# A two-layer transformer-and-SSM kernel: quantisation through PSUM ring banks, a router that reads PSUM, and a new table of slots

## The reference, cut to what matters

```
attention:  softmax((x*w_lhs) @ (x*w_rhs).T) @ x
fp8 layer:  x_q = (bf16(x) / s_in).astype(float8_e4m3fn)
            y   = (x_q @ k_q) * (s_in * s_k), in bf16, plus bias
SSM:        in_proj, causal convolution over 4 taps, silu,
            scan over 512 steps with 16 states for 512 channels, gate, out_proj
MoE:        scores = softmax(x @ gate_w.T) over 8 experts, the best 2 per token,
            their silu-gated products, weighted by the score,
            plus a shared expert times a sigmoid gate
```

## Time and profile before

| | us |
|---|---|
| median of 3 runs | 3776.05 (3775.61 to 3776.88) |
| the profiled execution, its own time | 3764.44 |
| its span, first to last instruction | 3762.7 |
| the first stage | until about 3030 |
| mean granted TensorE clock | 0.899 of full speed |

### The profile page before, as it was taken

How to read it: one execution, slowest core, us unless ns; L and a number is a source line. 1 busy time by engine, 2 the same in 40 slices (tenths; PEclk the granted TensorE clock), 3 DMA queues, 4 the chain that set the end, 5 groups by cost and what they waited for, 6 DMA issues and landing times. The chain is left out here.

```text
span 3762.7 us, 46426 instructions
## 1 busy us (share of the span) xinstructions
PE 2964.0 (79%) x12696; PEld 1908.2 (51%) x12697; DVE 2680.7 (71%) x4101; ACT 2032.6 (54%) x3738; POOL 2645.6 (70%) x2497
## 2 busy tenths in 40 slices
PE   3676868787877878787878696878687759999997
PEld 1444544554554545545454454554545436666665
DVE  2498898989898989898988888888988522222221
ACT  2566656666665657575656666656565313333332
POOL 1389887888888888888887878788899523333333
PEclk8897989889888989898989898989897879999998
DMA  2010111111111110101010101111011053333332
GB/s 67 21 32 28 38 35 36 35 34 37 34 35 34 37 40 31 43 30 41 28 43 32 40 32 37 35 37 36 30 39 37 25 148 55 53 53 53 53 53 44
DMA packets 113257, 155.35 MB, mean 41 GB/s; under 512 B 15601, under 2 KB 72369, under 8 KB 113073
## 3 DMA queue, kind: packets, MB, share of 16 engines
q1 hardware_dynamic: 72624, 99.79, 8.7%
q0 software_dynamic: 26112, 35.81, 5.5%
q10 hardware_dynamic: 14336, 17.57, 1.5%
HBM read 107.36 MB, written 45.76 MB: 41 GB/s over the span
## 5 line engine op out<-in xcount | busy, mean ns | idle before, releaser
L785 POOL TENSOR_TENSOR dbu<-du,bbc 128x512 f32<-128x512 f32 x1024 | 1298.3, 1280 | 129.2 <-DVE h L1269 120.1
L1269 DVE TENSOR_TENSOR_SCAN h<-bank,dbu 128x512 f32<-128x512 f32 x1024 | 1221.6, 1210 | 150.4 <-PE bank L609 67.2
L980 ACT ACTIVATE bank<-delta,amat 128x512 f32<-128x512 f32 x1024 | 704.2, 690 | 532.1 <-DVE h L1269 526.9
L609 PE MATMUL bank<-ident,h 128*128 128x128 f32 x4096 | 643.2, 294 | 403.2 <-DVE acc L1259 378.3
L609 PEld LDWEIGHTS bank<-ident,h 128*128 128x128 f32 x4096 | 512.7, 152 | 704.0 <-DVE acc L1259 366.1
L771 POOL TENSOR_TENSOR acc<-acc,hTc 128x512 f32<-128x512 f32 x480 | 611.2, 1273 | 184.8 <-ACT hTc L964 182.8
L1472 POOL DMA_INDIRECT out<-ye,ids x136 | 213.5, 1570 | 450.3 <-issue 236.1
L964 ACT ACTIVATE hTc<-bank,cT 128x512 f32<-128x512 f32 x480 | 326.9, 681 | 270.8 <-PE bank L609 268.5
L563 PE MATMUL bank<-x4T,w_su 128*128 128x512 f32 (+1 forms) x768 | 430.2, 656 | 0.0
L1519 DVE SCALAR_TENSOR_TENSOR gg<-gt,bank 128x352 f32<-128x352 f32 x136 | 70.9, 521 | 500.3 <-ACT gt L1422 500.3
L1259 DVE SCALAR_TENSOR_TENSOR acc<-bank,cT,acc 128x512 f32<-128x512 f32 x544 | 393.5, 728 | 18.4 <-PE bank L609 16.8
(11 more groups left out here) (197 smaller groups left out, 4522.3 us busy)
## 6 DMA issues: line engine op xcount, KB each, us to landing
bbc<-b_scratch SPq DMA_DIRECT2D x256, 256.0 KB, 3.1
xe<-slots_in SPq DMA_DIRECT2D x136, 129.0 KB
x<-in_x SPq DMA_DIRECT2D x16, 512.0 KB, 3.9
out<-x ACTq DMA_DIRECT2D x16, 512.0 KB, 3.0
w_gu<-in_e_gu ACTq DMA_DIRECT2D x8, 704.0 KB
out<-ye,ids POOLq DMA_INDIRECT x136, 3.8
slots_in<-x,pos POOLq DMA_INDIRECT x128
w_dn<-in_e_dn ACTq DMA_DIRECT2D x16, 128.0 KB
```

What stands on the lines that cost most here:

```text
L609: last = tr(scan[f"hT{s}.{t}"][:, m * P:(m + 1) * P], h[:, s % 2, m, t * P:(t + 1) * P], ident[:, :])
L785: g.tensor_tensor(dbu[:, n % 4, :], du[:, m, :], bbc[:, (b * NS + s) % NROW, :], ALU.mult).then_inc(S("dbu_ready"), 1)
L980: f(db(n)[:, :], delta[:, par, m, :], ACT.Exp, scale=amat[:, m, s:s + 1]).then_inc(S("da_ready"), 1)
L1269: v.tensor_tensor_scan(h[:, s % 2, m, :], db(n)[:, :], dbu[:, n % 4, :], 0.0, ALU.mult, ALU.add)\
```

## The change

- **Quantisation.** The working value `qm` lies in two ring banks, each with half of the tile; `reserve` takes them in TensorE's order at slot `q_dve` with no fill, `take` lets VectorE wait for their former readers. VectorE does each step in two halves of 128x512: exponent bits and magic (slot 57), then add and subtract in their new forms. ScalarE forms the overflow product from PSUM into SBUF (`q_nan`=56), and VectorE makes the last add into `qb` (`q_fin`=58). GpSimd has no part in it.
- **Router.** The logits are read from PSUM with no copy, the exponentials are written to another part of the same bank; the indices go to float by a reduction over one element instead of a cast; the running count starts from `run`, which is now row 0 of `cum`, so that its copy goes; the sums are written to the count's bank and cast from there. The logit bank is held until the scores, the count bank until the positions are made.
- **Slots.** The table `AT` is set anew, some forty entries, most by one or two slots.

```diff
+    def reserve(self, name, b):
+
+        self.free.sort()
+        bank = self.free.pop(0)[2]
+        turn, slot = self.due[name]
+        self.at[name, b] = (bank, self.fills[bank])
+        self.before[name, b] = self.last[bank]
+        self.free.append((b + turn, slot, bank))
+        self.last[bank] = (name, b)
+
+    def take(self, eng, name, b, done):
+
+        earlier = self.before[name, b]
+        if earlier:
+            for sem, i in self.readers[earlier[0]]:
+                done(eng, sem, earlier[1], i)
...
+        cum = psb("cum", [P, TT, E])
+        run = cum[:, 0, :]
...
-            yT=(0, 0, 1, 1), y=(1, 1, 1, 1), uD=(2, 2, 3, 3), acc0=(1, 2, 2, 3), out=(4, 6), x3=(8, 10), stats5=11, rstd5=11, x4=14,
-            x4T_pe=(14, 16), x4T=(15, 18), logit=18, lg=20, lexp=20, score=26, route=28, count=39, place=41,
-            ranks=(42, 43, 44, 45, 50, 51, 52, 53), g_pe=(20, 26, 30, 40, 44, 50), g=(22, 27, 32, 41, 46, 51),
-            gate=(24, 29, 34, 43, 48, 53), u_pe=(23, 26, 33, 42, 47, 54), up=(25, 29, 36, 45, 50, 54), d_pe=(51, 56), fin=(59, 66),
-            stats3=2, rstd3=1, res=3, r4=4, r4T_pe=5, r4T=4, in_x=(8, 10, 15, 17), tap=(11, 12, 17, 19), conv=(13, 15, 19, 21),
-            tanh=(13, 15, 20, 21), u=(16, 17, 22, 24), base=12, xBC_pe=24, bs=26, cT_pe=27, cT=32, in_z=(31, 38, 44, 51),
-            z=(34, 40, 47, 53), zs=(36, 41, 48, 55), dt_pe=(26, 34, 40, 46), raw=(30, 38, 44, 50), sp_exp=(32, 41, 46, 52), sp_ln=50,
-            delta=(53, 54, 55, 56), stats1=4, rstd1=4, xn=8, xT=(9, 12), xl=(11, 12), scores=(15, 19, 21, 26), maxs=(18, 21, 25, 29),
-            probs=(18, 21, 25, 29), probT_pe=(30, 33, 34, 35), probT=(32, 34, 36, 39), av=(40, 48), x1=(45, 53), stats2=47, rstd2=51,
-            xb=54, q=52, q_dve=56, q_add=56, qT_pe=61, qT=62, ffn_pe=(62, 63), ffn=(63, 64), x2=64, store=1, tags=(41, 50))
+            yT=(0, 0, 1, 2), y=(0, 0, 1, 1), uD=(2, 3, 3, 3), acc0=(1, 2, 2, 2), out=(4, 6), x3=(7, 10), stats5=12, rstd5=11, x4=14,
+            x4T_pe=(14, 16), x4T=(14, 16), logit=17, lg=20, lexp=20, score=21, route=26, count=39, place=40,
+            ranks=(42, 45, 45, 47, 50, 51, 52, 54), g_pe=(20, 26, 30, 40, 44, 50), g=(22, 27, 32, 41, 46, 51),
+            gate=(24, 29, 34, 43, 48, 53), u_pe=(23, 25, 33, 42, 44, 54), up=(25, 29, 36, 45, 51, 56), d_pe=(51, 56), fin=(58, 63),
+            stats3=2, rstd3=1, res=3, r4=4, r4T_pe=5, r4T=3, in_x=(8, 10, 15, 17), tap=(11, 12, 17, 19), conv=(13, 15, 19, 21),
+            tanh=(13, 15, 20, 21), u=(16, 17, 23, 24), base=12, xBC_pe=24, bs=25, cT_pe=29, cT=31, in_z=(31, 38, 45, 51),
+            z=(33, 40, 48, 53), zs=(38, 43, 50, 55), dt_pe=(26, 34, 40, 49), raw=(30, 38, 44, 52), sp_exp=(32, 44, 49, 55), sp_ln=51,
+            delta=(54, 55, 56, 56), stats1=4, rstd1=4, xn=8, xT=(9, 11), xl=(11, 12), scores=(15, 19, 21, 26), maxs=(18, 21, 25, 29),
+            probs=(18, 21, 24, 29), probT_pe=(30, 33, 34, 36), probT=(32, 34, 36, 37), av=(40, 47), x1=(46, 52), stats2=48, rstd2=51,
+            xb=54, q=50, q_dve=57, qT_pe=56, qT=62, ffn_pe=(63, 63), ffn=(63, 64), x2=64, store=0, tags=(40, 54), q_round=54, q_nan=56,
+            q_fin=58)
...
+        for k in range(2):
+            attn.add(f"qm{k}", -2, AT["q_fin"], ("q_ready", 0))
...
-        late.add("logit", 1, AT["lg"], ("lg_ready", 0))
-        late.add("count", 1, AT["place"], ("slot_ready", None))
+        late.add("logit", 1, AT["score"], ("score_ready", None))
+        late.add("count", 1, AT["place"], ("pos_ready", 0))
...
+        def router_views(b):
+
+            bank = late["logit", b]
+            return (bank[:, 0:TT * (E + 1)].rearrange("p (t e) -> p t e", e=E + 1),
+                    bank[:, P:P + TT * E].rearrange("p (t e) -> p t e", e=E))
...
+                yield AT["q_dve"]
+                for k in range(2):
+                    attn.reserve(f"qm{k}", b)
...
-                yield AT["q_add"]
-
-                done(pool, "q_nan", b)
-                g.tensor_tensor(qb[:, :, :], qm[:, :, :], qs[:, :, :], ALU.add).then_inc(S("q_ready"), 1)
...
+                yield AT["q_nan"]
+                done(act, "q_rounded", b)
+                for k in range(2):
+                    last = f(qm[:, 2 * k:2 * k + 2, :], attn[f"qm{k}", b][:, :].rearrange("p (j d) -> p j d", j=2), ACT.Copy, scale=3.4e38 / 460.0)
+                last.then_inc(S("q_nan"), 1)
...
+                    f(sg[:, :], given[:, :, E], ACT.Exp, scale=-1.0).then_inc(S("sg_ready"), 1)
                     f(lexp[:, :, :], lsub[:, :, :], ACT.Exp).then_inc(S("lexp_ready"), 1)
-                    f(sg[:, :], lg[:, :, E], ACT.Exp, scale=-1.0).then_inc(S("sg_ready"), 1)
...
-                names = SHARED["q_step"][1:]
-                to_e4m3(qs[:, :, :], qm[:, :, :], lambda n: done(dve, names[n], b), [S(n) for n in names])
+                quants = [(qs[:, 2 * k:2 * k + 2, :], attn[f"qm{k}", b][:, :].rearrange("p (j d) -> p j d", j=2),
+                           qm[:, 2 * k:2 * k + 2, :], qb[:, 2 * k:2 * k + 2, :]) for k in range(2)]
+                for k in range(2):
+                    attn.take(dve, f"qm{k}", b, done)
+                for q, m, _, _ in quants:
+                    last = v.tensor_scalar(m.bitcast(i32), q.bitcast(i32), 0x7F800000, None, ALU.bitwise_and)
+                last.then_inc(S("q_expo"), 1)
+                done(dve, "q_expo", b)
+
+                for q, m, _, _ in quants:
+                    last = v.tensor_scalar(m, m, 2.0 ** -6, 1.5 * 2.0 ** 20, ALU.max, ALU.mult)
+                last.then_inc(S("q_magic"), 1)
+                yield AT["q_round"]
+                done(dve, "q_magic", b)
+                for q, m, _, _ in quants:
+                    last = v.tensor_tensor(q, m, q, ALU.add)
+                last.then_inc(S("q_added"), 1)
+                done(dve, "q_added", b)
+                for q, m, _, _ in quants:
+                    last = v.scalar_tensor_tensor(m, m, -1.0, q, ALU.mult, ALU.add)
+                last.then_inc(S("q_rounded"), 1)
+                yield AT["q_fin"]
+                done(dve, "q_nan", b)
+                for q, m, big, rounded in quants:
+                    last = v.scalar_tensor_tensor(rounded, big, 0.0, m, ALU.mult, ALU.add)
+                last.then_inc(S("q_ready"), 1)
...
-                    v.tensor_copy(lg[:, :, :], late["logit", b][:, 0:TT * (E + 1)].rearrange("p (t e) -> p t e", e=E + 1)).then_inc(S("lg_ready"), 1)
-                    done(dve, "lg_ready", b)
-                    v.tensor_reduce(lmax[:, :], lg[:, :, 0:E], AX.X, ALU.max).then_inc(S("lmax_ready"), 1)
+                    v.tensor_reduce(lmax[:, :], given[:, :, 0:E], AX.X, ALU.max).then_inc(S("lmax_ready"), 1)
                     done(dve, "lmax_ready", b)
-                    v.tensor_tensor(lsub[:, :, :], lg[:, :, 0:E], lmax[:, :].unsqueeze(2).broadcast_to([P, TT, E]), ALU.subtract)\
+                    v.tensor_tensor(lsub[:, :, :], given[:, :, 0:E], lmax[:, :].unsqueeze(2).broadcast_to([P, TT, E]), ALU.subtract)\
...
-                    v.tensor_copy(f8[:, :, :], i8[:, :, :]).then_inc(S("idxf_ready"), 1)
+                    v.tensor_reduce(f8[:, :, :], i8[:, :, 0:2].unsqueeze(3), AX.X, ALU.max).then_inc(S("idxf_ready"), 1)
...
-                    v.tensor_copy(cum[:, 0, :], run[:, :]).then_inc(S("cum0"), 1)
+                    if b > 0:
+                        done(dve, "run_ready", b - 1)
                     for j in range(1, TT):
-                        done(dve, f"cum{j - 1}", b)
-                        v.tensor_tensor(cum[:, j, :], cum[:, j - 1, :], tiles[:, j - 1, :], ALU.add).then_inc(S(f"cum{j}"), 1)
+                        if j > 1:
+                            done(dve, f"cum{j - 1}", b)
+                        v.tensor_tensor(cum[:, j, :], tiles[:, j - 1, :], cum[:, j - 1, :], ALU.add).then_inc(S(f"cum{j}"), 1)
                     done(dve, f"cum{TT - 1}", b)
-                    v.tensor_tensor(run[:, :], cum[:, TT - 1, :], tiles[:, TT - 1, :], ALU.add).then_inc(S("run_ready"), 1)
-                    v.tensor_tensor(slot[:, :, :], cum[:, :, :], within, ALU.add).then_inc(S("slot_ready"), 1)
+                    v.tensor_tensor(slot[:, :, :], within, cum[:, :, :], ALU.add).then_inc(S("slot_ready"), 1)
                     done(dve, "slot_ready", b)
+                    v.tensor_tensor(run, tiles[:, TT - 1, :], cum[:, TT - 1, :], ALU.add).then_inc(S("run_ready"), 1)
                     v.tensor_tensor(ohb[:, :, :, :], ohb[:, :, :, :], slot[:, :, :].unsqueeze(1).broadcast_to([P, 2, TT, E]), ALU.mult)\
                         .then_inc(S("prod_ready"), 1)
                     done(dve, "prod_ready", b)
-                    v.tensor_reduce(posf[:, :, :], ohb[:, :, :, :], AX.X, ALU.add).then_inc(S("posf_ready"), 1)
+                    posf = late["count", b][:, P:P + 2 * TT].rearrange("p (w t) -> p w t", w=2)
+                    v.tensor_reduce(posf, ohb[:, :, :, :], AX.X, ALU.add).then_inc(S("posf_ready"), 1)
```

(2 more changed lines are left out.)

22 lines of the change are left out of this document (11 added, 11 removed).

## The result

The kernel after the change takes 3544.85 us (median of 4 runs, 3531.26 to 3554.79) beside 3775.83 us of the kernel before: 0.939 times, 95% interval 0.9356 to 0.9425. The profiled execution of after has a span of 3542.6 us, against 3762.7: 220.1 us less.

A forecast was written before the change was run, and what follows sets the result against it. VectorE was taken as the bound, 87% busy in a 180.8 us turn. Terms 70 - 1 + 40 + 37 = 146 us, less 14, gave 132 off 3764.4, 3632; plus 11.6, 3644 us, range 3590 to 3730.

The forecast's parts named there:

- Gain 5.4 us a turn: Quantisation on VectorE: 11.7 us removed, 6.3 us added per turn; over 13 turns 70 us, less 1 at the start.
- The last add leaving GpSimd: Quantisation: GpSimd loses its add of 2.34 us; not taken as a gain of its own, bounds 0 and 2.34.
- The other shifts: Slots: z and zs two slots later, y at 0, touch waits of 1.7 us and less; nothing taken.
- I take off a tenth: Whole sum: some freed time will end at GpSimd's adds, with GpSimd 86% busy; 14 us taken off 146.
- The late up product: Slots: VectorE's 4.89 us wait for TensorE's last up product; about half saved, 2.5 us x 15 turns = 37 us.
- the forecast's second remark: Slots: the last softplus exponential moves to 55, putting ScalarE's logarithm block under VectorE's quantisation; laid bare it costs 72 us.
- The router: Router copies and casts removed or reading PSUM: 3.1 us a turn, 2.5 taken, x 16 = 40 us, bounds 0 and 50.
- first rival: The holds move to VectorE instructions with two SBUF inputs: router gains nothing, 74 us in all, 3702 us; chance 0.10.
- Second rival: Slower: in-order stall as TensorE waits at slot 57 for the quantised tile; in full 3840 us; chance 0.07.
- Fourth: PSUM at single rate, no hold lifted: 22 us dearer, router 0, 3761 us, or no change; chance 0.05.
- more than forecast, all upper bounds: Whole kernel: every term at its upper bound, time below 3590 us; chance 0.03.
- The bounds of the terms: Largest gains allowed: quantisation 107 us, router 50 us, slots 99 us (6.6 us a turn).

The follow-up runs named there:

- q_only: The kernel before with only the quantisation's new code, router and slots as they were; 3680.27 us, ratio 0.9756.
- score21: The kernel before with only the score's slot moved from 26 to 21; 3728.75 us, ratio 0.9875.
- r_only: The kernel before with the router's new code and the score's slot moved from 26 to 21; 3694.54 us, ratio 0.9794.
- qr_oldslots: The kernel before with the new quantisation and router code on the old slots, with the edits of q_only and r_only; 3585.33 us, ratio 0.9501.
- q_hold: q_only with the quantisation's first pass as before, one instruction from SBUF to SBUF; 3767.26 us, ratio 0.998.
- qr_up: qr_oldslots with the last two up products moved from slots 50 and 54 to 51 and 56; 3615.36 us, ratio 0.9571.
- qr_tail: qr_up with the last softplus exponential moved from slot 52 to 55, its product and raw copy to 49 and 52; 3593.59 us, ratio 0.9526.
- s_only: The kernel before with only the new slots, quantisation and router code as before; 3644.43 us, ratio 0.9661.
- place_only: The kernel before with only the second half of the router's code (running counts and positions); 3726.1 us, ratio 0.9869.
- rest_only: The kernel after with the last up products, last softplus exponential, its product and raw copy back on old slots; 3627.88 us, ratio 0.9617.
- after_hold: The kernel after with the quantisation's first pass as before, one instruction from SBUF to SBUF; 3544.55 us, ratio 0.9401.

## Why the prediction was wrong

The sign and the main mechanism, the lifted hold, were right, the size was not. The sum goes against the runs as follows, in the order in which the forecast built it; measured numbers are medians, the first two against before in their batches, the next three as differences of such gains.

| term | forecast us | measured us | from |
|---|---|---|---|
| quantisation, old slots | 69 | 93 | q_only |
| score's slot | 0 | 46 | score21 |
| router's code | 40 | 33 | r_only less score21 |
| together more, or less | -14 | 16 | qr_oldslots less the two |
| other slots | 37 | 43 | after less qr_oldslots |
| sum | 132 | 231 | |

By the intervals of the runs the measured differences are good to some 12 us each. Three steps failed: the score's slot was put at nothing and gave 46 us; a tenth was taken off where the parts together gave more than apart; and the quantisation, priced by its own passes' rows, gave 93 us for 69.

**The quantisation**, "Gain 5.4 us a turn": right in its cause, and q_hold shows that cause; the size was 6.8. The passes cost 6.4 us, as costed (6.3), and by VectorE's rows they gave about what was forecast (69 us): 172.1 us in before, 105 in q_only. The step that failed is the one that gave the part no worth beyond the passes' own rows. Other passes from SBUF to SBUF became shorter by some 15 us in all, above all the bias add (26.1 to 19.8 us) and the sum at the edge of the convolution (18.2 to 12.0), first in before, then in q_only:

```profile
L1092 DVE TENSOR_TENSOR r4T<-r4T,fbias 128x1024 bf16<-128x1024 bf16 x16 | 26.1, 1633 | 14.6 <-ACT r4T L843 14.6
...
L1106 DVE TENSOR_TENSOR cs<-cs,edge 128x3 f32<-128x3 f32 x64 | 18.2, 284 | 10.5 <-ACT cs L872 10.4
```

```profile
L1139 DVE TENSOR_TENSOR r4T<-r4T,fbias 128x1024 bf16<-128x1024 bf16 x16 | 19.8, 1234 | 9.7 <-ACT r4T L866 9.7
...
L1153 DVE TENSOR_TENSOR cs<-cs,edge 128x3 f32<-128x3 f32 x64 | 12.0, 187 | 10.7 <-ACT cs L895 10.5
```

That the other engines had run dry behind the hold gave little: VectorE's idle time is 23.6 us a turn in before and 22.7 in q_only. The last add leaving GpSimd, costed at nothing, was worth little on the old slots: all but 7 us of the 93, give or take 10, is the hold.

**The slots**, "The other shifts [...] touch waits of 1.7 and less; nothing taken": this is the largest miss, 46 us. The score's slot was not costed at all. By the change's diff it moves, and it stands ahead of L1188 and L1192, two passes whose rows were on the table with holds of 0.74 and 0.44 us in them; score21 shows both gone. The forecast asked of each held pass what form it would have, and not when it would run.

**"I take off a tenth"** stood for GpSimd becoming the bound. It did not: GpSimd is at 147.0 us of a 163.9 us turn, 90% busy, and the scans wait for it for 1.6 us in a turn of after. In place of -14 stood +16, give or take 12. The sum was built from VectorE's busy rows, and its idle time is where the parts gain together: by the profiled spans idle time falls by 5.5 us in q_only, 17.4 in r_only, 51.1 in qr_oldslots and 115.0 in after. TensorE's granted clock goes the same way, 0.899 in before's profiled run, 0.908, 0.901, 0.922 and 0.921 in these.

**The late up product** was forecast at "about half of 4.9". The wait did go, and the forecast's second remark, that the logarithms have to go under the quantisation at the same time, is borne out in part: qr_up, which leaves it out, is 30 us slower, but qr_tail, which has it, only comes level with the old slots. The size of 37 came out near 43, but through a table that can't be split, and as 63.9 us less idle and 27.2 us more busy time than in qr_oldslots, so this agreement is in part luck and weak support.

**The router**, 2.5 us a turn: 33 us measured on top of the score's slot, 49 for its second half without it. Right in size; its claim to the cast's 0.74 us overlaps with the slot.

**The rivals.** The holds did move in part (L1162, L1272, L1245, against before's 0.28, 0.35 and 0.23 us each), first rival: 64 x 0.34 + 16 x 0.34 + 16 x 0.32 = 32 us of busy time, inside a total that still fell by 105. Second rival: TensorE's wait at the quantised tile is 2.0 us, far from the 8 that was to show it. VectorE's waits ahead of the sums into `acc` did grow by 22 us in all, but s_only, where TensorE comes to the tile at 61 as before, has them too (41.0 us), so they are not this wait's. Fourth: PSUM at the single rate with no hold lifted is refuted by q_only and q_hold. The Trainium skill (VectorE: DVE Perf Modes, Why PSUM operands drop a tier) holds in its number: 1.26 to 1.30 us for a pair with PSUM beside 0.67 to 0.69 in one piece. It doesn't tell the time of the kernel.

**The range.** The case "more than forecast, all upper bounds", below 3590, had 0.03, and it came. The bounds of the terms add up to 107 + 50 + 99 = 256 us, so the 231 measured lie inside them: the parts were 93, 79 with the score's slot, 16 together and 43. What was wrong is the chance. It took the terms as if one could not help another: VectorE had 23.6 us of idle time a turn, and the bounds drew on it only for 6.6 us at two waits.

What stays open: why the score's earlier slot saves 46 us when VectorE's busy time fell by 22; the rest is idle time that I can't trace to one wait (ahead of the scans 27.5 us less, ahead of the gate 12.1 less, ahead of the attention maxima 11.4 more, ahead of the up products 9.6 more). Also why place_only gives 49 us for 30 us of rows, and why passes far from an edit, as the bias add, become shorter. Holding the count bank longer may reorder the banks; no run has that hold alone. And it stays open how much of the idle time gained is TensorE's higher clock and how much comes first and raises it: among the four runs of after alone, the one at 0.916 took 3554.79 us and the one at 0.924 took 3531.26.

## What to carry to other kernels

When VectorE's row has instructions ten times longer than their shape allows, look at what GpSimd does under them: either their operands (one in PSUM) or their place (in this kernel, where GpSimd issues transfers instead of computing) can free them, and the two gains don't add. A form with an operand in PSUM can be worth having beside a busy GpSimd for GpSimd's sake, with VectorE's own time unchanged. Where slots are set by hand in one table, cost every slot that the diff moves, and don't expect half a new schedule to give half its gain: rest_only is worse than the old slots and the new.

## What the runs showed of the hardware

- A held one-input pass from SBUF to SBUF waited for six GpSimd instructions in a row, 7.1 us, until they paused. The Trainium skill (SBUF — State Buffer, Who interferes with whom) says that the one who issues first has the shared pair "for the whole instruction"; the trace shows a wait of several instructions, so back-to-back GpSimd work counts as one. The Trainium skill's other sentence in that section, that issue order decides and not the shape, does not tell the two cases here apart: by the profile's times the GpSimd instruction starts first in both, by 0.14 to 0.17 us in after_hold (0.67 us) and by 0.02 to 0.18 in q_hold (7.76 us). What differs is what it is.
- Beside a GpSimd instruction that issues an indirect transfer (0.96 us), the one-input pass ran unheld, at 0.67 us from start to end inside it, in 12 of 12 turns of s_only and of after_hold.
- Passes with both inputs in SBUF and GpSimd's own slow each other: 2.18 us for 1.23, and 2.25 for 1.27. With one input in PSUM neither changes (1.29 and 1.30 us a pair, 1.27 and 1.26 us on GpSimd).
- VectorE writing PSUM costs no more than reading it: 0.68 us for 128x512 with the input in SBUF and the result in PSUM (L1125), 0.69 with both in PSUM (L1130) and 0.69 from PSUM to SBUF (L1135).
